# A hypergraph layer's node table that begins as a copy of x, and Newton's roots on VectorE in the node stage

## The chip, the cores and the metric

The kernel runs on one core of a Trainium2 chip. The metric is the device time of one execution in microseconds, lower is better; it is taken as the median of several runs. Engines: TensorE (PE), VectorE (DVE), ScalarE (ACT), GpSimd (POOL) and SyncE (SP). SP issues plain DMAs; POOL issues the indirect ones, which gather, scatter or add rows by an index. All of them are carried out by the core's 16 DMA engines, SP's on queue q1 and POOL's on queue q0 of the profile.

## The reference

Four graph layers stand in a row over 50,000 nodes of 256 float32 features and 25,000 edges, each with a residual and a layer norm. The change lies in the first of them, the hypergraph layer, and in the norm behind it:

```python
def _layer(x, node_idx, edge_idx, norm_n2e, norm_e2n, W_n2e, W_e2n):
    h = x @ W_n2e
    msg = norm_n2e[:, None] * h[node_idx]
    e = jax.ops.segment_sum(msg, edge_idx, num_segments=NUM_EDGES)
    e = jax.nn.relu(e)
    h2 = e @ W_e2n
    msg2 = norm_e2n[:, None] * h2[edge_idx]
    n = jax.ops.segment_sum(msg2, node_idx, num_segments=NUM_NODES)
    return (n, e)
...
Dn_inv = jnp.where(Dn > 0, 1.0 / Dn, 0.0)
norm_e2n = Dn_inv[node_idx]
x1, _ = _layer(x, node_idx, edge_idx, norm_n2e, norm_e2n, W0_n2e, W0_e2n)
x1 = jax.nn.relu(x1)
x2, _ = _layer(x1, node_idx, edge_idx, norm_n2e, norm_e2n, W1_n2e, W1_e2n)
...
x = _layernorm(x + _L0_gnn_ref(x, edge_index, ...), axis=-1)
```

So a node's value after the block is the norm of x plus the sum of its messages in the second layer, divided by the number of its edges.

## The kernel before

`hyper_layer_phase` does one hypergraph layer and runs twice, as e0 and e1. The edges lie as 128 partitions of 196 columns, J = 4 columns to a tile, so 49 tiles.

The **upward pass** takes one tick per tile. POOL gathers the source rows of four columns (L792) into g, which holds eight tiles. In e1 the rows come from the node table NS0 and carry, behind 256 features, the count of their edges; DVE's `scale` turns the count into its inverse, `inv`, in two alternating buffers, and multiplies the rows (L863 to L870). DVE's `accumulate` then runs sums of equal targets through the columns (L885), in three buffers `run`, and SP stores each finished tile (L1119). Ahead of each store SP issues clears of the node table that the layer will add into: `clear_rows` writes zeros from SBUF, 520 KB each; e1 does its 100 clears of NS1 in this way. DVE may overwrite a buffer of `run` once its store has landed, and POOL may gather into g once the tile of eight ticks before is summed.

The **downward pass** takes one tick for two columns: two products and a relu, the sums of rows with an equal source by a matmul into `pa`, ACT's copy of them into `tot` (L1080), and POOL's two indirect adds of `tot` into the node table (L822). The adds of one pair are issued when those of the pair before have landed. A row of the table is SW = 260 floats: 256 of sums, then the count. Beside the adds POOL gathers two columns of indices per tick (L832). ACT also waits for adds before it writes `tot` again, and then evicts the next product into `o` (L1089).

`first_nodes_phase`, the **node stage** (tag n0), goes over the 98 tiles of 512 nodes. Per tile SP loads the rows of x into `a` (L1201) and the rows of NS1 into `r` (L1202). DVE takes the inverse of the count (L1311, L1314), adds sums times inverse to the rows (L1319, four times), and takes row statistics (L1326). Once per two tiles it joins them into mean and variance (L1300, L1306), POOL takes the variance to the power of -0.5 (L1217), and DVE makes the shift (L1293). ACT normalises into `o` (L1269), TensorE turns the rows (L1237) and multiplies them by a weight (L1247), DVE evicts the product with a row added (L1285), and POOL scatters four times 128 rows of 2112 bytes to XH (L1223). The stages of one tile lie a fixed number of ticks apart. Every engine goes through its own instructions in program order.

Later layers of the kernel have a row norm of their own in which DVE takes the roots by Newton's steps (L2509 to L2519).

Of the kernel before, what the change touches and what calls it, by code (L numbers as in the profile page):

```python
# [5 lines left out]
F32 = mybir.dt.float32  # L6
# [6 lines left out]
P = 128  # L13
# [4 lines left out]
J = 4  # L18
# [153 lines left out]
def clear_rows(eng, table, zero, n, sem):  # L172

    eng.dma_start(table.rearrange("(p r) c -> p r c", p=P)[:, n * CLEAR:(n + 1) * CLEAR, :], zero[:]).then_inc(sem, 16)

# [508 lines left out]
def hyper_layer_phase(nc, S, tag, table, tw, sums, w1, w2, nodes, clear, up, scatter=None, listing=None, homes=None, gather=None, early=None):  # L684
# [7 lines left out]
    scaled = tw > D  # L692
    with Scope(nc, tag) as s:
# [18 lines left out]
        tot = [s.sb(f"tot{b}", [P, 2, SW]) for b in range(2)]  # L712
# [67 lines left out]
        with s.block() as block:  # L780

            @block.gpsimd
            def _(pool):
# [29 lines left out]
                for tick in range(down_ticks):  # L813
                    q = pair(tick, ADD)
                    if q:
                        pool.wait_ge(s_cp, q)
                        if q == 1:
                            pool.wait_ge(clear, 16 * CLEARS)
                        else:
                            pool.wait_ge(s_add, 32 * (q - 1))  # L820
# [18 lines left out]
            def _(dve):  # L839
# [19 lines left out]
                def scale(t):  # L859
                    gt, iv = g[:, t % RG * J:(t % RG + 1) * J, :], inv[t % 2]  # L860
                    dve.wait_ge(s_g[t % RG], 16 * J * (t // RG + 1))
                    scale_lk.settle(dve)
                    scale_lk.link(dve.tensor_scalar(iv[:], gt[:, :, D], 1.0, None, ALU.max))  # L863
                    yield
                    scale_lk.settle(dve)
                    scale_lk.link(dve.reciprocal(iv[:], iv[:]))
# [128 lines left out]
            def _(pe):  # L995
# [10 lines left out]
                for tick in range(down_ticks):  # L1006
                    q = pair(tick, SUM)
                    if q:
# [5 lines left out]
                        pe.matmul(pa[:, 0, 0:SW], e[:, 0, :], mt[:, 0, :], start=True, stop=False)  # L1014
                        pe.matmul(pa[:, 0, 0:SW], e[:, 2, :], mt[:, 1, :], start=False, stop=True)
                        pe.matmul(pa[:, 1, 0:SW], e[:, 1, :], mt[:, 1, :], start=True, stop=True).then_inc(s_tot, 1)
# [52 lines left out]
            def _(act):  # L1069
# [3 lines left out]
                for tick in range(down_ticks):  # L1073
                    q = pair(tick, COPY)
                    if q:
# [4 lines left out]
                        act.activation(tot[q % 2][:], pa[:, :, 0:SW], ACT.Copy).then_inc(s_cp, 1)  # L1080
# [27 lines left out]
            def _(sp):  # L1108
                if home:
                    home.load(sp)  # L1110
                for tick in range(up_ticks):
                    if tick < TR:
                        nodes_of, sem, n0, n1 = up
                        for n in range(n0 + (n1 - n0) * tick // TR, n0 + (n1 - n0) * (tick + 1) // TR):
                            clear_rows(sp, nodes_of, S["zero"], n, sem)
# [23 lines left out]
def first_nodes_phase(nc, S, A, T):  # L1139
# [3 lines left out]
    LD, ADD, VAR, NORM, TURN, ZT, PROD, EVICT, STORE = 0, 2, 3, 5, 6, 7, 8, 9, 10  # L1143
    RA, RR, RO = 7, 4, 7
    with Scope(nc, tag) as s:
        a = [s.sb(f"a{b}", [P, J, D]) for b in range(RA)]
        r = [s.sb(f"r{b}", [P, J, SW]) for b in range(RR)]
        o = [s.sb(f"o{b}", [P, J, XW]) for b in range(RO)]
        inv = [s.sb(f"inv{b}", [P, J]) for b in range(2)]
# [4 lines left out]
        nb = [s.sb(f"nb{b}", [P, 2 * J]) for b in range(2)]  # L1154
        zt = [s.sb(f"zt{b}", [P, KC, J, P]) for b in range(2)]
# [3 lines left out]
        s_rin = s.sems("sums_loaded", RR)  # L1159
        s_clr = s.sem("cleared")  # L1160
        s_u = s.sem("sum_ready")
# [9 lines left out]
        count_lk = Links(s.sem("count_steps"))  # L1171
# [1546 lines left out]
```

## Time and profile before

| | |
|---|---|
| median of 3 runs | 6743.85 us (6737.83 to 6748.29) |
| span of the profiled execution | 6891.4 us; no other time is given for that execution |
| busy share of the span | PE 62%, DVE 69%, ACT 48%, POOL 58% |
| DMA | 1634.06 MB, 237 GB/s over the span |
| upward pass of e1 | about 1148 to 1452 us |
| downward pass of e1 | about 1500 to 2200 us |
| node stage | about 2208 to 2860 us |

All times of the profile come from one profiled execution, whose span is 2.2% above the median of the runs. The busy share of the whole span says little here, since the stages follow one another and each has its own limit. What counts is read stage by stage: which engine or queue has no free time there.

### The profile page before, as it was taken

Reading aid. Unit: us, or ns where it says so; the run is one execution under the profiler, and the core shown is the slowest. Engines: PE = TensorE matmul, PEld = TensorE weight load, DVE = VectorE, ACT = ScalarE, POOL = GpSimd, SP = SyncE. Lnnn points to the kernel's source line nnn. Section 1 sums busy time; section 2 is a strip of 40 time slices with the busy share of each in tenths; the row PEclk is TensorE's granted clock in tenths of the full one; section 3 lists DMA queues with packets and bytes.
Section 4 is the critical chain, followed back from the end, with each engine's and each line's share of the span. In section 5 each row is a group of like instructions: output and inputs, shape, how many; then the busy total and the mean of one; then the engine's idle time right before and its main releaser. Section 6 shows DMA issues by size and latency. Waiting matters only on the chain. (4 is left out here: it accounts for less than half of the span.)

```text
span 6891.4 us, 79060 instructions
## 1 busy us (share of the span) xinstructions
PE 4257.5 (62%) x18989; PEld 3141.2 (46%) x18989; DVE 4783.1 (69%) x15487; ACT 3305.7 (48%) x7376; POOL 4010.9 (58%) x3167
## 2 busy tenths in 40 slices
PE   2568883038885788499866677988885677600000
PEld 1247773037774666377612223547774566500000
DVE  6635544645454877599599996866665999587666
ACT  0023331013332555288656665758885788633333
POOL 4757776757775788767155426611113666277776
PEclk9779996569998999799978778989998899855555
DMA  7845445864544999799688988989996677477665
GB/s 278 287 121 79 76 75 147 335 197 75 79 76 89 328 350 351 219 326 342 200 293 304 312 273 318 379 290 328 331 336 222 231 258 247 175 261 242 236 227 193
DMA packets 646111, 1634.06 MB, mean 237 GB/s; under 512 B 128454, under 2 KB 283878, under 8 KB 630290
## 3 DMA queue, kind: packets, MB, share of 16 engines
q1 hardware_dynamic: 459954, 1234.83, 51.9%
q0 software_dynamic: 185696, 394.18, 21.4%
q8 instruction: 157, 2.57, 0.2%
q14 instruction: 304, 2.49, 0.1%
HBM read 816.50 MB, written 813.62 MB: 237 GB/s over the span
## 5 line engine op out<-in xcount | busy, mean ns | idle before, releaser
L822 POOL DMA_INDIRECT NS<-e_tot,e_idx x392 | 648.6, 1655 | 298.1 <-ACT e_tot L1080 222.4
L2304 ACT ACTIVATE l_z<-l_a,l_nb,l_rs 128x256 f32<-128x256 f32 x1176 | 612.7, 605 | 411.3 <-DMA out_dram<-l_z,k_ids 248.1
L1691 POOL DMA_INDIRECT l_eg<-HBT,k_nsrc x392 | 461.8, 1178 | 391.2 <-DVEq L1916 151.3
L956 DVE TENSOR_SCALAR e_eq<-e_pk,z_skey 128x128 f32<-128x128 f32 x588 | 204.2, 348 | 637.1 <-DMA NS<-e_tot,e_idx 608.1
L2181 POOL DMA_INDIRECT out_dram<-l_z,k_ids x392 | 432.0, 1102 | 150.9 <-issue 115.1
L1734 PE MATMUL l_pb<-l_jx,k_ones 128*128 128x128 f32 x26 | 4.3, 304 | 788.3 <-DVE l_jx L1971 788.3
L1080 ACT ACTIVATE e_tot<-e_pa 128x520 f32<-128x520 f32 x196 | 118.6, 605 | 759.7 <-DMA NS<-e_tot,e_idx 748.6
L2226 PE MATMUL l_pm<-k_w_L3b,l_zt 128*128 128x258 f32 x1568 | 404.5, 417 | 126.8 <-ACT l_o L2274 121.8
L2475 DVE BATCH_NORM_STATS2 l_bs<-l_a 128x6 f32<-128x256 f32 x1176 | 467.2, 420 | 10.5 <-issue 3.5
L1223 POOL DMA_INDIRECT XH<-n_o,z_home x392 | 398.0, 1015 | 118.1 <-issue 113.1
L2342 ACT ACTIVATE l_a<-l_a,l_eshare 128x64 f32<-128x64 f32 (+1 forms) x1372 | 382.0, 371 | 124.4 <-DVE l_eshare L1953 67.6
L1911 DVE SCALAR_TENSOR_TENSOR l_erun<-l_erun,k_same,l_eg 128x260 f32<-128x260 f32 (+2 forms) x880 | 422.9, 481 | 19.2 <-DMA l_r<-XH 12.0
L2200 PE MATMUL l_ps<-l_a,k_ident 128*128 128x512 f32 x392 | 288.1, 825 | 235.0 <-DVE l_a L2449 206.5
L2226 PEld LDWEIGHTS l_pm<-k_w_L3b,l_zt 128*128 128x128 f32 x1568 | 320.6, 210 | 189.0 <-issue 138.2
L1247 PE MATMUL n_pm<-z_w_L1a,n_zt 128*128 128x264 f32 x1568 | 398.7, 411 | 12.5 <-DVE n_o L1285 12.3
L2226 PE MATMUL l_pm<-k_w_L1b,l_zt 128*128 128x264 f32 x1568 | 377.8, 395 | 26.0 <-ACT l_o L2274 25.9
L1440 POOL TENSOR_TENSOR n_rs<-n_ve,k_minus_half 128x8 f32<-128x8 f32 x49 | 80.2, 1638 | 538.4 <-DVE n_ve L1559 538.4
L2174 POOL TENSOR_TENSOR l_rs<-l_ve,k_minus_half 128x8 f32<-128x8 f32 x98 | 196.6, 2006 | 338.1 <-DVE l_ve L2499 220.3
L1031 PE MATMUL e_po<-z_w_e2n,e_hid 128*128 128x256 f32 x1584 | 381.4, 384 | 13.5 <-DVEq L919 13.5
L1691 POOL DMA_INDIRECT l_eg<-HA,k_nsrc x196 | 290.6, 1483 | 162.0 <-DVEq L1916 67.3
L1040 PE MATMUL e_pr<-e_zt,z_w_n2e 128*128 128x256 f32 x1584 | 379.6, 383 | 1.5 <-issue 1.1
L1691 POOL DMA_INDIRECT l_eg<-XH,k_psrc x196 | 299.9, 1530 | 125.9 <-DVEq L1916 66.4
(409 smaller groups left out, 13538.8 us busy)
## 6 DMA issues: line engine op xcount, KB each, us to landing
NS<-z_zero SPq DMA_DIRECT2D x200, 520.0 KB
HBT<-l_o SPq DMA_DIRECT2D x196, 528.0 KB
l_a<-HBT SPq DMA_DIRECT2D x196, 528.0 KB
GSUMS<-l_erun SPq DMA_DIRECT2D x72, 1056.0 KB
l_a<-XH SPq DMA_DIRECT2D x98, 528.0 KB
HA<-n_o SPq DMA_DIRECT2D x98, 528.0 KB
l_a<-HA SPq DMA_DIRECT2D x98, 528.0 KB
n_r<-NS SPq DMA_DIRECT2D x98, 520.0 KB
```

Of the source, the lines that this page charges most:

```text
L822: pool.indirect_dma_start(out=nodes, out_offset=bass.IndirectOffsetOnAxis(ap=idx[q % DEEP][:, k:k + 1], axis=0), in_=tot[q % 2][:, k, :], ...
L1031: mm = pe.matmul(po[:, k, :], hid[q % 2][:, i, k * P:(k + 1) * P], w2[:, i, 0:D], start=i == 0, stop=i == KC - 1)
L1040: mm = pe.matmul(pr[:, n, :], w1[:, i, n * P:(n + 1) * P], zt[q % 2][:, i].rearrange("p j n -> p (j n)"), start=i == 0, stop=i == KC - 1)
L1223: pool.indirect_dma_start(out=T["XH"], out_offset=bass.IndirectOffsetOnAxis(ap=S["home32"][:, col:col + 1], axis=0), in_=o[t % RO][:, j, : ...
L1247: last = pe.matmul(pm[h][:, i, 0:RW], zt[t % 2][:, k, h * (J // 2) + i, :], weight[:, k, :], start=k == 0, stop=k == KC - 1)
L1691: pool.indirect_dma_start(out=self.g[b % self.ng][:, k, :], out_offset=None, in_=self.table, in_offset=bass.IndirectOffsetOnAxis(ap=self.i ...
L1911: lk.link(dve.scalar_tensor_tensor(rt[:, k, 0:n], before, S["same"][:, b * BC + k:b * BC + k + 1], g[:, k, 0:n], ALU.mult, ALU.add))
L2181: pool.indirect_dma_start(out=self.out, out_offset=bass.IndirectOffsetOnAxis(ap=S["ids32"][:, col:col + 1], axis=0), in_=self.z[u % self.r ...
L2226: last = pe.matmul(self.pm[h][:, i, 0:self.wc], zt[:, k, h * (J // 2) + i, :], self.weight[:, k, 0:self.wc], start=k == 0, stop=k == KC - 1)
L2304: last = act.activation(z[:, j, 0:D], a[:, j, 0:D], ACT.Identity, bias=self.nb[b][:, col:col + 1], scale=self.rs[b][:, col:col + 1])
L2342: last = act.activation(a[:, j, f], a[:, j, f], ACT.Copy, scale=sh[:, 0, t % 2 * J + j, h:h + 1])
L2475: self.stat_lk.link(dve.bn_stats(bs[:, u % 2 * J + j, :], a[:, j, 0:D]))
```

## The change

There are two edits. First, the node table of the second hypergraph layer, NS1, has rows of 256 floats instead of 260, and it begins as x instead of as zeros: during e1's upward pass SP copies x into it (`copy_rows`, 98 DMAs from DRAM to DRAM) and clears only the spare rows. The totals are multiplied by the inverse count on ACT before they are added, in two activations instead of one, for which `inv` is kept for all tiles. So the table already holds x plus the scaled sums. The node stage then loads one tile instead of two and has no inverse and no add. Second, POOL's power leaves the node stage: DVE takes the root with a first guess and four Newton steps, thirteen dependent operations on 128x8, in a tick of their own (ROOT). The stage has one tick more from load to store, nine buffers `a` instead of seven and eight `o` instead of seven.

```diff
+def copy_rows(eng, table, x, n, sem):
+    if n == TAILN:
...
+    else:
+        eng.dma_start(table[n * BLK:(n + 1) * BLK, :].rearrange("(p j) w -> p (j w)", j=J),
+                      x[n * BLK:(n + 1) * BLK, :].rearrange("(p j) w -> p (j w)", j=J)).then_inc(sem, 16)
...
+def clear_spare_rows(eng, table, zero, sem):
+    spare = NPAD - 2 * P
+    eng.dma_start(table[spare:NPAD, :].rearrange("(p j) w -> p j w", j=2), zero[:, 0:2, 0:D]).then_inc(sem, 16)
+    eng.dma_start(table[N:N + P, :], zero[:, 0, 0:D]).then_inc(sem, 16)
...
-        inv = [s.sb(f"inv{b}", [P, J]) for b in range(2)]
+        inv = s.sb("inv", [P, TR, J]) if scaled else None
...
-                        act.activation(tot[q % 2][:], pa[:, :, 0:SW], ACT.Copy).then_inc(s_cp, 1)
+                        if scaled:
+                            for k in range(2):
+                                c = column(q) + k
+                                last = act.activation(tot[q % 2][:, k, :], pa[:, k, 0:ow], ACT.Copy, scale=inv[:, c // J, c % J:c % J + 1])
...
                         for n in range(n0 + (n1 - n0) * tick // TR, n0 + (n1 - n0) * (tick + 1) // TR):
-                            clear_rows(sp, nodes_of, S["zero"], n, sem)
+                            if x is None:
+                                clear_rows(sp, nodes_of, S["zero"], n, sem)
+                            else:
+                                copy_rows(sp, nodes_of, x, n, sem)
...
-    LD, ADD, VAR, NORM, TURN, ZT, PROD, EVICT, STORE = 0, 2, 3, 5, 6, 7, 8, 9, 10
-    RA, RR, RO = 7, 4, 7
+    LD, STAT, VAR, ROOT, SHIFT, NORM, TURN, ZT, PROD, EVICT, STORE = 0, 2, 3, 4, 5, 6, 7, 8, 9, 10, 11
+    RA, RO = 9, 8
...
-                            sp.dma_start(a[t % RA][:], A["x"][t * BLK:(t + 1) * BLK, :].rearrange("(p j) w -> p j w", j=J)).then_inc(s_in[t % RA], 16)
-                        sp.dma_start(r[t % RR][:], T["NS1"][t * BLK:(t + 1) * BLK, :].rearrange("(p j) w -> p j w", j=J)).then_inc(s_rin[t % RR], 16)
+                            sp.dma_start(a[t % RA][:], T["NS1"][t * BLK:(t + 1) * BLK, :].rearrange("(p j) w -> p j w", j=J)).then_inc(s_in[t % RA], 16)
...
-                        pool.tensor_tensor(rs[b][:], ve[b][:], S["minus_half"][:, 0:w], ALU.pow).then_inc(s_rs, 1)
...
+                def root(q):
...
+                    root_lk.settle(dve)
+                    root_lk.link(dve.tensor_scalar(y[:].bitcast(I32), v[:].bitcast(I32), -0.5, float(0x5F3759DF), ALU.mult, ALU.add))
+                    yield
+                    for n in range(4):
+                        root_lk.settle(dve)
+                        root_lk.link(dve.tensor_tensor(w[:], y[:], y[:], ALU.mult))
+                        yield
+                        root_lk.settle(dve)
+                        root_lk.link(dve.scalar_tensor_tensor(w[:], w[:], -0.5, v[:], ALU.mult, ALU.mult))
+                        yield
+                        root_lk.settle(dve)
+                        ins = dve.scalar_tensor_tensor(y[:], w[:], 1.5, y[:], ALU.add, ALU.mult)
...
-                def add(t):
-                    at, rt, iv = a[t % RA], r[t % RR], inv[t % 2]
...
-                        last = dve.scalar_tensor_tensor(at[:, j, :], rt[:, j, 0:D], iv[:, j:j + 1], at[:, j, :], ALU.mult, ALU.add)
...
-        "NS1": nc.dram_tensor("NS1", (NPAD, SW), F32).ap(),
+        "NS1": nc.dram_tensor("NS1", (NPAD, D), F32).ap(),
```

SP's instructions at the start of e1's upward pass, before the change (NS is a node table, SUMS the table of stored runs; the first row loads an index table):

```order
L577 DMA e_raw<-META 128x400
L174 DMA NS<-z_zero 128x1040 x10
L1119 DMA SUMS<-e_run 128x1024
L174 DMA NS<-z_zero 128x1040 x2
L1119 DMA SUMS<-e_run 128x1024
```

The same place after the change:

```order
L593 DMA e_raw<-META 128x400
L189 DMA NS<-z_zero 256x1x256
L190 DMA NS<-z_zero 128x256
L182 DMA NS<-in_x_dram 16x8192 x10
L1148 DMA SUMS<-e_run 128x1024
L182 DMA NS<-in_x_dram 16x8192 x2
L1148 DMA SUMS<-e_run 128x1024
```

The copies take exactly the places of the clears, two ahead of each store, and each is laid out as 16 pieces of 8192 floats, where a clear had 128 of 1040.

DVE's instructions in one tick of the node stage before the change, one in which the variance of a pair of tiles is made (n_o is the output tile, n_bs and n_mv the row statistics, n_ve the variance, n_a the rows):

```order
L1285 TENSOR_TENSOR n_o<-n_pm,z_row_a 128x2x264
L1300 BN_AGGR n_mv<-n_bs 128x2 x2
L1311 TENSOR_SCALAR n_inv<-n_r 128x4
L1285 TENSOR_TENSOR n_o<-n_pm,z_row_a 128x2x264
L1300 BN_AGGR n_mv<-n_bs 128x2 x2
L1314 RECIPROCAL n_inv<-n_inv 128x4
L1300 BN_AGGR n_mv<-n_bs 128x2 x2
L1319 SCALAR_TENSOR_TENSOR n_a<-n_r,n_inv,n_a 128x256
L1300 BN_AGGR n_mv<-n_bs 128x2 x2
L1319 SCALAR_TENSOR_TENSOR n_a<-n_r,n_inv,n_a 128x256
L1306 TENSOR_SCALAR n_ve<-n_mv 128x8
L1319 SCALAR_TENSOR_TENSOR n_a<-n_r,n_inv,n_a 128x256 x2
```

DVE in a tick of the node stage after the change, one of those with a root (n_rs is the root, n_sq its scratch):

```order
L1299 TENSOR_TENSOR n_o<-n_pm,z_row_a 128x2x264
L1318 TENSOR_SCALAR n_rs<-n_ve 128x8
L1351 BN_STATS n_bs<-n_a 128x6
L1299 TENSOR_TENSOR n_o<-n_pm,z_row_a 128x2x264
L1322 TENSOR_TENSOR n_sq<-n_rs 128x8
L1351 BN_STATS n_bs<-n_a 128x6
L1325 SCALAR_TENSOR_TENSOR n_sq<-n_sq,n_ve 128x8
L1351 BN_STATS n_bs<-n_a 128x6
L1328 SCALAR_TENSOR_TENSOR n_rs<-n_sq,n_rs 128x8
L1351 BN_STATS n_bs<-n_a 128x6
L1322 TENSOR_TENSOR n_sq<-n_rs 128x8
L1325 SCALAR_TENSOR_TENSOR n_sq<-n_sq,n_ve 128x8
```

The adds and the inverse are gone. The root's steps alternate with evictions and statistics as long as there are some; the last nine of the thirteen follow one another directly (two of them are shown). On POOL the 49 powers between every eight scatters of the stage are gone, and its 392 scatters follow one another.

## Rows read from the trace of the kernel before

**Rows 1.** Busy time by stretch: PE, PEld, DVE, ACT, POOL, clock, DMA share, GB/s.

```profile
1148.00:1452.00 304.00, 1.80 (x4) 1.01 (x4) 192.74 (x573) 0.00 (x0) 212.47 (x199) 0.50 0.91 346
1500.00:2200.00 700.00, 582.37 (x2908) 495.13 (x2908) 343.70 (x1767) 236.61 (x486) 506.94 (x368) 0.97 0.47 72
2300.00:2750.00 450.00, 366.48 (x1760) 300.45 (x1758) 355.68 (x1250) 229.64 (x441) 362.62 (x331) 0.93 0.98 350
```

**Rows 2.** Timeline of POOL, node stage: the first and the last scatter.

```profile
2259.07 1.06 POOL L1223 DMA_INDIRECT XH<-n_o,z_home  x1 [0.18 <-issue]
...
2854.88 0.97 POOL L1223 DMA_INDIRECT XH<-n_o,z_home  x1 [0.30 <-issue]
```

**Rows 3.** Groups of instructions, 2300 to 2750: busy us, mean ns, idle before.

```profile
L1223 POOL DMA_INDIRECT XH<-n_o,z_home x294 | 299.6, 1019 | 85.3 <-issue 84.6 <-ACT n_o L1269 0.5 <-DVE n_o L1285 0.2
L1217 POOL TENSOR_TENSOR n_rs<-n_ve,k_minus_half 128x8 f32<-128x8 f32 x37 | 63.6, 1718 | 2.4 <-issue 1.4 <-DVE n_ve L1306 0.5
...
L1319 DVE SCALAR_TENSOR_TENSOR n_a<-n_r,n_inv,n_a 128x256 f32<-128x256 f32 x292 | 126.6, 476 | 1.3
L1285 DVE TENSOR_TENSOR n_o<-n_pm,z_row_a 128x528 f32<-128x528 f32 x147 | 103.3, 703 | 90.5 <-PE n_pm L1247 48.3 <-remote 25.1 <-issue 17.0
L1311 DVE TENSOR_SCALAR n_inv<-n_r 128x4 f32<-128x4 f32 x73 | 11.9, 163 | 0.0
L1314 DVE RECIPROCAL n_inv<-n_inv 128x4 f32<-128x4 f32 x73 | 11.5, 157 | 0.0
```

**Rows 4.** Timeline of TensorE in the node stage, at full clock.

```profile
2519.59 3.73 PE L1247 MATMUL n_pm<-z_w_L1a,n_zt 128*128 128x264 f32 x16
...
2524.30 3.73 PE L1247 MATMUL n_pm<-z_w_L1a,n_zt 128*128 128x264 f32 x16
```

**Rows 5.** Timeline of POOL, downward pass: first add of three pairs.

```profile
1698.74 1.76 POOL L822 DMA_INDIRECT NS<-e_tot,e_idx  x1 [0.52 <-ACT e_tot L1080]
...
1705.62 1.76 POOL L822 DMA_INDIRECT NS<-e_tot,e_idx  x1 [0.49 <-ACT e_tot L1080]
...
1713.15 1.62 POOL L822 DMA_INDIRECT NS<-e_tot,e_idx  x1 [1.15 <-ACT e_tot L1080]
```

**Rows 6.** DMA queues, 1262 to 1355 (93 us): packets, MB, share of 16 engines.

```profile
q1 hardware_dynamic: 7982, 29.36, 78.6%
q0 software_dynamic: 3141, 8.72, 23.8%
```

**Rows 7.** DMA queues, node stage, 2300 to 2750.

```profile
q1 hardware_dynamic: 21186, 77.75, 53.7%
q0 software_dynamic: 23450, 79.29, 43.8%
```

**Rows 8.** Groups of DVE, 6000 to 6600: Newton's steps in a later layer.

```profile
L2516 DVE SCALAR_TENSOR_TENSOR l_rt<-l_rt,l_ve 128x8 f32<-128x8 f32 x128 | 20.9, 163 | 10.5 <-DVE l_rt L2513 4.4 <-issue 2.9 <-remote 1.9
L2513 DVE TENSOR_TENSOR l_rt<-l_rs 128x8 f32<-128x8 f32 x128 | 20.8, 163 | 18.1 <-remote 10.9 <-DVE l_rs L2519 5.7
L2519 DVE SCALAR_TENSOR_TENSOR l_rs<-l_rt,l_rs 128x8 f32<-128x8 f32 x128 | 20.8, 162 | 16.9 <-remote 9.3 <-DVE l_rt L2516 6.2
...
L2509 DVE TENSOR_SCALAR l_rs<-l_ve 128x8 int32<-128x8 int32 x32 | 6.4, 201 | 11.2 <-issue 11.2
```

**Rows 9.** Timeline, start of the node stage: the last memset of `a`.

```profile
2216.67 0.91 DVE L1278 MEMSET n_a<- 128x1024 f32 x1 [0.16 <-issue]
```

**Rows 10.** Groups of ACT, downward pass, 1500 to 2200.

```profile
L1089 ACT ACTIVATE e_o<-e_po,z_einv_end 128x256 f32<-128x256 f32 x196 | 82.3, 471 | 65.2 <-DVEq L934 51.3 <-PE e_po L1031 10.5 <-issue 3.4
L1080 ACT ACTIVATE e_tot<-e_pa 128x520 f32<-128x520 f32 x98 | 59.3, 605 | 378.4 <-DMA NS<-e_tot,e_idx 372.8 <-PE e_pa L1016 5.6
```

**Rows 11.** Waits of ACT and of POOL, 1500 to 2200: total, times, longest.

```profile
ACT e_o L1089 <- DVEq L934: 51.3, 89, 1.1
...
POOL NS L822 <- ACT e_tot L1080: 106.1, 87, 27.4
```

**Rows 12.** DMA queue of the adds and index gathers, 1600 to 2100.

```profile
q0 software_dynamic: 25186, 19.11, 36.4%
```

More of the change, by code:

```diff
@@ L711, in hyper_layer_phase @@
         idx = [s.sb(f"idx{b}", [P, 2], I32) for b in range(DEEP)]
-        tot = [s.sb(f"tot{b}", [P, 2, SW]) for b in range(2)]
+        tot = [s.sb(f"tot{b}", [P, 2, ow]) for b in range(2)]
         pt = [s.ps(f"pt{b}", [P, KC, 2, P]) for b in range(2)]
@@ L1112, in _ @@
                     if tick < TR:
-                        nodes_of, sem, n0, n1 = up
+                        nodes_of, sem, n0, n1, x = up
+                        if x is not None and tick == 0:
+                            clear_spare_rows(sp, nodes_of, S["zero"], sem)
                         for n in range(n0 + (n1 - n0) * tick // TR, n0 + (n1 - n0) * (tick + 1) // TR):
-                            clear_rows(sp, nodes_of, S["zero"], n, sem)
+                            if x is None:
+                                clear_rows(sp, nodes_of, S["zero"], n, sem)
+                            else:
+                                copy_rows(sp, nodes_of, x, n, sem)
                     t = tile(tick, 4)
@@ L1154, in first_nodes_phase @@
         nb = [s.sb(f"nb{b}", [P, 2 * J]) for b in range(2)]
+        sq = [s.sb(f"sq{b}", [P, 2 * J]) for b in range(2)]
         zt = [s.sb(f"zt{b}", [P, KC, J, P]) for b in range(2)]
@@ L1208, in _ @@
                 for tick in range(ticks):
-                    q = pair(tick, VAR)
-                    if q is not None:
-                        q, w = q
-                        b = q % 2
-                        pool.wait_ge(s_var, q + 1)
-                        if q >= 2:
-                            pool.wait_ge(s_nb, q - 1)
-                            pool.wait_ge(s_z, 2 * (q - 1))
-                        pool.tensor_tensor(rs[b][:], ve[b][:], S["minus_half"][:, 0:w], ALU.pow).then_inc(s_rs, 1)
                     t = tile(tick, STORE)
@@ L1332, in _ @@
                         parts.append(evict(tick - EVICT))
-                    q = pair(tick - 1, VAR)
+                    q = pair(tick, SHIFT)
                     if q is not None:
                         parts.append(shifts(q[0]))
+                    q = pair(tick, ROOT)
+                    if q is not None:
+                        parts.append(root(q[0]))
                     q = pair(tick, VAR)
@@ L1338, in _ @@
                         parts.append(variance(*q))
-                    if tile(tick, ADD) is not None:
-                        parts.append(add(tick - ADD))
+                    if tile(tick, STAT) is not None:
+                        parts.append(stats(tick - STAT))
                     take_turns(parts)
```

61 lines of the change are left out of this document (30 added, 31 removed).

## The prediction

> **What bounds the kernel now.** I began with the busy time by stretch, to separate the three stages that the change touches [rows 1]. In the row 1148 to 1452 (upward pass of the second hypergraph layer) TensorE does nothing and the DMA engines are 91% busy at 346 GB/s. In 1500 to 2200 (its downward pass) they are 47% busy and TensorE 83%. In 2300 to 2750 (the middle of the node stage) they are 98% busy at 350 GB/s. The three stages have three different limits.
>
> In the node stage a tile's pace comes from the first and the last scatter of POOL: from 2259.07 to 2854.88 us there are 391 intervals, so 595.8 / 391 x 4 = 6.095 us for a tile of four scatters [rows 2]. POOL has no free time in it. Its scatters follow one another after 0.30 us that wait for nothing ("issue"), and once per pair of tiles a power of 1.7 us stands between them, with 0.18 behind it, as before the first scatter: 1.88 us a pair. Over 2300 to 2750 the groups say the same: 299.6 + 85.3 us for 294 scatters and 63.6 + 2.4 for the powers are 450.9 of 450 us [rows 3]. ACT's wait for a scatter to land is the stage backing up behind POOL and the DMA engines. So two limits lie on each other here: POOL's own work, and DMA at 98%. TensorE is behind them: at full clock one tile's products start 4.71 us after the last tile's (2519.59, 2524.30) [rows 4].
>
> In the downward pass POOL issues two adds into the table and two small gathers for each pair of columns: 1698.74 to 1705.62 is 6.88 us with 0.49 us of gap before the next pair's first add, and sometimes the adds of the pair before land late and the gap is 1.15 us [rows 5]. In the upward pass the DMA engines are the limit where it runs well: in 1262 to 1355 they move 410 GB/s, and the two data queues together take 102% of them [rows 6].
>
> **The change, node stage: fewer loads, no power on POOL.** Of each tile's three streams one goes, the 520 KB load of sums. The queue q1 took 53.7% of 16 engines for 450 us to move 77.75 MB, and the scatters' q0 43.8% for 79.29 MB [rows 7]. That is 0.537 x 7200 / 77.75 = 49.7 engine-us per MB to load and 39.8 to store. A tile now needs 0.52 MB of loads and 1.08 MB of scatters: (26.1 + 43.0) / 16 = 4.3 us. DMA is out of the way. POOL loses 1.88 / 2 = 0.94 us per tile; what stays is four scatters, 4 x (0.97 + 0.30) = 5.08 at the undisturbed length and 4 x (1.019 + 0.30) = 5.28 at the mean that a full DMA system gives [rows 2, 3]. I take 5.2.
>
> Does VectorE allow that? It was busy 355.7 us for 73.7 tiles, 4.83 us each [rows 1]. Out go four adds (0.476 us by the group; four in a row took 1.67 in the timeline) and the count's two small operations (0.32, of which about 0.1 lies on neighbours): about 1.9. In come thirteen dependent operations on 128x8 per pair of tiles. The layers later in the program run the same chain, so its price is in the trace: 20.9 + 20.8 + 20.8 + 6.4 us busy, and 10.5 + 18.1 + 16.9 + 11.2 us idle before them, for 32 pairs, is 125.6 / 32 = 3.9 us per pair, 1.95 per tile [rows 8]. Sum 4.83 - 1.9 + 1.95 = 4.9 us, just under POOL's 5.2. The order above shows that the last nine of these operations stand alone, with nothing to fill the waits between them; without any waits (13 x 0.163 = 2.1 per pair) VectorE would need 4.0, so 4.0 to 4.9. TensorE's 4.71 fits too; where its clock falls (0.93 on average in rows 1) it needs 4.71 / 0.93 = 5.06. Everything is within 0.5 us of the same pace, which is why I don't go below 5.2.
>
> Term one: (6.095 - 5.2) x 97.75 tiles = -87. Against it, about +4: two more of the 0.91 us memsets ahead of the first load, each with 0.16 before it [rows 9], and a first pass that is one tick deeper, whose chain of 3.9 stands in place of 1.7. Node stage: **-83 us**.
>
> **Downward pass.** ACT writes the totals in two activations of 128x256 instead of one of 128x520. Two such back to back are in the trace as the evictions at line 1089, 0.471 each by the group, so 0.94 at most in place of 0.605, +0.34 us [rows 10]. ACT then waits for DVE 0.58 us at a time anyway (51.3 us in 89 times) before its next work [rows 11], and POOL needs this copy only one pair later. I cost it at nothing; with that cover gone it would be 98 x 0.34 = +33. The added rows shrink from 1040 to 1024 bytes. POOL's issue doesn't depend on that as far as any row shows. What could gain is the landing: POOL waited 106.1 us in 87 times, 27.4 of it once at the start, so 0.92 each for the rest, against the 0.49 of rows 5 where POOL came from other work; at most 0.43 x 86 = -37. I take **-5**, a seventh, since most pairs in rows 5 are POOL's own work.
>
> **Upward pass: clears become copies.** This is the term on which the sign hangs. 100 clears of 520 KB from SBUF become 98 copies of 512 KB from DRAM to DRAM, and two small clears of 262 and 131 KB. As the order shows, each copy is 16 pieces of 32 KB, one per engine, on SP's queue, two ahead of each store of runs. Stores wait behind copies in that queue, VectorE waits for stores after three tiles, and POOL for VectorE after eight. So nothing defers them past the stage.
>
> Price of a clear now: in rows 6 q1 took 0.786 x 1488 / 29.36 = 39.8 engine-us per MB, so 0.5325 x 39.8 / 16 = 1.33 us of all engines; 100 are 133. Price of a copy: the trace has none. From below, it can't be cheaper than the store leg alone, 0.524 x 39.8 / 16 = 1.31. From above, if the engine does its read leg and then its write leg, at the node stage's rates, (49.7 + 39.8) x 0.524 / 16 = 2.93. Only the adds into the table read DRAM and write it in one packet, with 1040-byte rows: they look dear (36.4% of 8000 engine-us for 19.11 MB, 152 per MB, four times a store [rows 12]), but they also read a second source and come in small rows, so they bound nothing above; they only say that the cheap end is not to be assumed. I take 2.4: two store legs (2.62) with a little overlap. Then 98 x 2.4 = 235, less 133: +102 us of DMA time. The stage has 9% of 304 us idle [rows 1], 27 us, into which the excess spreads since loads run up to eight tiles ahead: **+75 us**.
>
> The Trainium skill has a figure against this part: DMA: Bandwidth & Descriptors, Latency and other measured facts, gives copies between HBM tensors as 207 to 214 GB/s per direction at their full rate. By an estimate from that figure a copy is 2.45 us and the sum 5 us higher than mine. No row of this trace shows a DRAM-to-DRAM copy.
>
> **Sum.** -83 - 5 + 75 = -13 on a profiled span of 6891.4 us, which is 2.2% above the median of the runs, 6743.85; no separate time of the profiled execution is given. Scaled or not, that is -13: 6730 us. A measurement of this kernel tells 0.2%, 13.5 us, from no change.
>
> **Rivals.**
> (1) The two halves nearly cancel, the forecast: a copy at 2.2 to 2.65, node pace 5.1 to 5.4. Stage +55 to +100, node -63 to -92: 6690 to 6775. Chance 0.50.
> (2) The copy is nearly as cheap as a clear, at 1.31 to 1.8 us: reads and writes overlap in an engine. For it: q1's loads and stores use the same engines at 50 and 40, no engine shows a second limit. Stage -5 to +16, so 6640 to 6675. Chance 0.32.
> (3) The other side: read leg and write leg in turn, 2.93 us. 98 x 2.93 - 133 = 154 of DMA time, less 27: +127, sum +39: 6783. It decides from the price at which 98 x - 160 = 88, that is 2.53 us, and is measurably slower from 2.67. Its place is SP's queue, where run stores stand behind copies. Chance 0.12.
> (4) VectorE bounds the node stage: the lone chain costs 3.9 us per pair on top of evictions that wait on TensorE, pace 5.7. Node -35, sum +35: 6779. For it: VectorE's evictions already wait for TensorE in rows 3 (48.3 us). Against: those waits are slack in a stage that POOL holds back. Chance 0.06.
>
> **The numbers.** In (1) the centre is at -13, so about half lies below -13.5, a third within, a sixth above. Faster: 0.32 + 0.23 = 0.55 less 0.03 for (2) meeting (4), 0.52. Within 0.2%: 0.18. Slower: 0.30. The range that leaves out 2 in 10 is 6650 to 6785; (1) alone has 6690 to 6775.
>
> **What would show it.** The first scatter to the last, 391 intervals, should be 508 us (5.2 a tile), POOL's idle still "issue", DMA share about 0.83 and VectorE about 4.9 us per tile. The upward pass should last about 380 us rather than 304, with DMA near 1.0 throughout and q1 at 73 engine-us per MB on copies. The adds of the downward pass should keep their 6.9 us. I am wrong if the upward pass keeps its length (rival 2), passes 430 us (3), or if POOL waits for VectorE in the node stage (4).

## The result and the profile after

The changed kernel took 6634.14 us (median of 4 runs, 6632.3 to 6637.03) against 6743.44 us before: ratio 0.9832, 95% interval 0.9818 to 0.9846. The forecast was 6730, range 6650 to 6785. So 109 us were gained where 13 were forecast. The experiments added a limit to this: on two other chips, where the kernel before takes 6872 and 6885 us, the changed kernel is no faster at all (last section).

The profile shown ahead of the prediction has a span of 6891.4 us, 2.2% above its median. A second profile of the kernel before, `before_again` (span 6727.6), is used for differences. It was taken later than the profile after, in the session of the first experiments, whose kernel before took 6738.19 us. By stage, first to last instruction of its kind, in us:

| stage | before_again | after | difference | forecast |
|---|---|---|---|---|
| e1 upward pass (first gather to last run) | 276.9 | 276.2 | -0.7 | +75 |
| e1 downward pass (adds) | 667.1 | 669.8 | +2.7 | -5 |
| first memset of `a` to first scatter | 48.2 | 35.5 | -12.7 | +4 |
| first to last scatter of the node stage | 594.2 | 504.4 | -89.8 | -87 |
| everything before e1's upward pass | | | +8 | 0 |
| everything from the next layer's first gather | 3974.9 | 3972.4 | -2.6 | 0 |

The spans differ by 93.9 us. The +8 ahead of the upward pass is no effect of the change: `copy_only` and `double_copy`, which have the same code up to there as after, begin that pass at 1092.5 and 1095.9 us, after at 1102.0 and before_again at 1094.3. The busy time by stretch (columns as in [rows 1]) of the kernel after, for the upward pass, the downward pass and the middle of the node stage:

```profile
1102.00:1378.00 276.00, 0.59 (x2) 0.50 (x2) 187.19 (x572) 0.00 (x0) 209.77 (x199) 0.50 0.99 375
1500.00:2100.00 600.00, 493.90 (x2480) 419.64 (x2478) 296.65 (x1529) 220.34 (x500) 452.77 (x329) 0.98 0.47 72
2300.00:2600.00 300.00, 269.95 (x1406) 227.71 (x1405) 228.33 (x1022) 182.52 (x349) 229.11 (x233) 0.98 0.90 306
```

The same three stretches in before_again:

```profile
1094.00:1371.00 277.00, 0.59 (x2) 0.50 (x2) 187.02 (x572) 0.00 (x0) 210.21 (x199) 0.50 0.99 379
1500.00:2100.00 600.00, 488.48 (x2436) 413.69 (x2434) 292.65 (x1510) 197.83 (x408) 447.80 (x325) 0.97 0.48 71
2300.00:2600.00 300.00, 242.75 (x1167) 200.41 (x1168) 235.18 (x824) 151.19 (x292) 241.65 (x220) 0.93 0.98 347
```

The upward pass has the same length and the same DMA share, 0.99, with copies as with clears, and the GB/s differ by no more than the bytes (512 KB a piece of work for 520). The DMA queues between 1150 and 1350 say it directly (packets, MB, share of 16 engines; compare [rows 6]); first after, then before_again:

```profile
q1 hardware_dynamic: 7629, 57.94, 71.5%
q0 software_dynamic: 7080, 19.53, 29.3%
```

```profile
q1 hardware_dynamic: 15555, 57.22, 71.3%
q0 software_dynamic: 7105, 19.63, 28.9%
```

Half the packets, the same bytes, the same share. 0.715 x 3200 / 57.94 = 39.5 engine-us per MB, copies and stores mixed, where the prediction had 73 for copies. The packet records of the two traces agree: a copy's 32768-byte packet takes 1214 ns (median of 1552), a clear's 4160-byte one 161 ns, which is 27.0 and 25.8 bytes per ns. All packets of the 97 full copies together took 125.5 us of 16 engines, 1.29 us a copy.

In the node stage POOL's scatters of after, the first and the last (timeline; they answer to [rows 2]):

```profile
2149.87 1.04 POOL L1237 DMA_INDIRECT XH<-n_o,z_home  x1 [44.83 <-DVE n_o L1299]
...
2654.27 0.98 POOL L1237 DMA_INDIRECT XH<-n_o,z_home  x1 [0.30 <-issue]
```

That is 504.4 / 391 x 4 = 5.16 us a tile. The groups of POOL and of VectorE in after, 2300 to 2600 (columns as in [rows 3]):

```profile
L1237 POOL DMA_INDIRECT XH<-n_o,z_home x233 | 229.5, 985 | 71.0 <-issue 66.4 <-DVE n_o L1299 4.6
```

```profile
L1299 DVE TENSOR_TENSOR n_o<-n_pm,z_row_a 128x528 f32<-128x528 f32 x117 | 82.6, 706 | 63.7 <-PE n_pm L1261 63.3
L1339 DVE BATCH_NORM_AGGREGATE n_mv<-n_bs 128x2 f32<-128x6 f32 x238 | 27.7, 159 | 0.0
L1328 DVE SCALAR_TENSOR_TENSOR n_rs<-n_sq,n_rs 128x8 f32<-128x8 f32 x116 | 19.2, 165 | 3.0
L1325 DVE SCALAR_TENSOR_TENSOR n_sq<-n_sq,n_ve 128x8 f32<-128x8 f32 x116 | 18.9, 163 | 3.0
L1322 DVE TENSOR_TENSOR n_sq<-n_rs 128x8 f32<-128x8 f32 x116 | 18.6, 160 | 2.0
...
L1318 DVE TENSOR_SCALAR n_rs<-n_ve 128x8 int32<-128x8 int32 x29 | 5.8, 200 | 0.0
```

POOL's 229.5 + 71.0 us fill the 300. It waits for VectorE for 4.6 us only. VectorE still waits 63.3 us for TensorE. Its Newton chain costs 62.5 us busy and 8 idle for 29 pairs, 2.4 us a pair.

### The profile page after: what moved, and what is told of

The parts are those of the page before. It is cut to its first block and busy times, and to the rows that moved or that the text cites. A ratio compares the mean times of both kernels' runs of the same rounds, so it can differ in the third digit from the quotient of the medians.

```text
span 6633.7 us, 78919 instructions
## 1 busy us (share of the span) xinstructions
PE 4192.1 (63%) x18989; PEld 3106.0 (47%) x18989; DVE 4681.3 (71%) x15539; ACT 3316.8 (50%) x7474; POOL 3866.4 (58%) x3118
## 5 line engine op out<-in xcount | busy, mean ns | idle before, releaser
L2209 POOL DMA_INDIRECT out_dram<-l_z,k_ids x392 | 417.8, 1066 | 119.6 <-issue 113.5
L1719 POOL DMA_INDIRECT l_eg<-HA,k_nsrc x196 | 271.6, 1386 | 177.8 <-DVEq L1944 86.8
L1261 PE MATMUL n_pm<-z_w_L1a,n_zt 128*128 128x264 f32 x1568 | 367.2, 388 | 0.0
L1499 PE MATMUL n_pm<-k_w_L3a,n_zt 128*128 128x264 f32 x1568 | 364.8, 386 | 0.0
```

The source lines that it names most:

```text
L1261: last = pe.matmul(pm[h][:, i, 0:RW], zt[t % 2][:, k, h * (J // 2) + i, :], weight[:, k, :], start=k == 0, stop=k == KC - 1)
L1719: pool.indirect_dma_start(out=self.g[b % self.ng][:, k, :], out_offset=None, in_=self.table, in_offset=bass.IndirectOffsetOnAxis(ap=self.i ...
L2209: pool.indirect_dma_start(out=self.out, out_offset=bass.IndirectOffsetOnAxis(ap=S["ids32"][:, col:col + 1], axis=0), in_=self.z[u % self.r ...
```

## The experiments

Each run is compared with the kernel before on its own chip; "us a tile" is the pace of the node stage's scatters. The first four ran on a chip whose kernel before took 6738.19 us; the changed kernel was not timed there.

**before_again**, the kernel before once more:

> The unchanged kernel of before, to have a profile whose span fits its time: the first profile had a span of 6891 us against a median of 6744, the changed kernel's 6634 against 6634. Theory: the first profiled execution was a disturbed one and this one shows about 6742 us, with the 150 us gone from all stages a little, among them the slow stretches at 1200 to 1262 and 1355 to 1390 us of the upward pass. With them gone that pass should take about 270 to 285 us and the node stage keep 6.1 us per tile. Rival: the profiler itself lengthens this kernel, and the span is again near 6890.

6729.27 us. The theory held: the upward pass took 276.9 us, the node stage 6.08 us a tile. It supplied the columns above.

**root_only**: the kernel before with the Newton root alone; both loads, the inverse and the adds stay.

```diff
-    LD, ADD, VAR, NORM, TURN, ZT, PROD, EVICT, STORE = 0, 2, 3, 5, 6, 7, 8, 9, 10
-    RA, RR, RO = 7, 4, 7
+    LD, ADD, VAR, ROOT, SHIFT, NORM, TURN, ZT, PROD, EVICT, STORE = 0, 2, 3, 4, 5, 6, 7, 8, 9, 10, 11
+    RA, RR, RO = 8, 4, 7
...
-                        pool.tensor_tensor(rs[b][:], ve[b][:], S["minus_half"][:, 0:w], ALU.pow).then_inc(s_rs, 1)
...
+                        parts.append(root(q[0]))
```

> Before, with the roots of the node stage on VectorE and nothing else changed (second load, adds, clears as before). Theory of two limits on each other: POOL has 0.94 us less per tile, but the DMA engines still need their 5.9 us for it, so the pace falls from 6.1 to 5.9 or 6.0: 10 to 15 us faster, 6730. Rival, POOL alone was the limit: pace 5.2 and 85 us faster, 6658. A third: VectorE, which keeps its adds (4.83 us) and gets the chain (1.95), is the limit at 6.8: 65 us slower.

6661.35 us, ratio 0.9883 (0.9864 to 0.9901). The scatters took 522.0 us, 5.34 a tile, 72 less than before, with as many bytes per tile. Its stretch 2300 to 2600, and POOL's only group there:

```profile
2300.00:2600.00 300.00, 262.51 (x1348) 218.87 (x1349) 297.13 (x1323) 176.64 (x339) 229.64 (x225) 1.00 1.02 401
```

```profile
L1216 POOL DMA_INDIRECT XH<-n_o,z_home x225 | 231.0, 1026 | 70.7 <-issue 70.7
```

The rival "POOL alone was the limit" (6658) came within 4 us, and the theory of two limits missed by 69 us. The same DMA engines that were 98% busy at 347 GB/s now move 401 GB/s. So a share of 98% in before was no limit, and POOL's power held the stage. VectorE is busy 297 of 300 us, and POOL's scatters with their gaps are 301.7: here both are at their end.

**copy_only**: the changed kernel with the root back on POOL.

```diff
+                        pool.tensor_tensor(rs[b][:], ve[b][:], S["minus_half"][:, 0:w], ALU.pow).then_inc(s_rs, 1)
...
-                        parts.append(root(q[0]))
```

> After, with the power back on POOL: only the copy, the scaled totals and the single load of the node stage. Theory of two limits: POOL needs 4 x 1.285 + 0.94 = 6.08 us per tile, as before, so the node stage gains nothing, and the whole change less this is 5 to 15 us faster than before (6730 to 6738), from the upward pass. Rival, the DMA engines alone were the limit: pace 5.2, 90 us faster.

6696.28 us, ratio 0.994 (0.9921 to 0.9958). Neither theory had this: the one of two limits expected no gain in the node stage and at least 6730 us, its rival 90 us. Scatters 573.9 us, 5.87 a tile; from memset to first scatter 37.9 us where root_only has 48.5. POOL's groups, 2300 to 2600:

```profile
L1246 POOL DMA_INDIRECT XH<-n_o,z_home x204 | 200.2, 982 | 59.2 <-issue 58.0 <-ACT n_o L1292 0.6 <-DVE n_o L1308 0.6
L1240 POOL TENSOR_TENSOR n_rs<-n_ve,k_minus_half 128x8 f32<-128x8 f32 x25 | 42.2, 1687 | 0.3
```

The scatter falls from 1030 ns in before_again to 982: one load less is worth 0.05 us per scatter, 0.2 a tile (20 us), and a fill that is 10 us shorter. The two edits alone give -77 and -42 us here; together they gave -109 by the medians of the first measurement, 10 less than the sum.

**double_copy**: every copy is issued a second time, into a table that nobody reads.

```diff
                                 copy_rows(sp, nodes_of, x, n, sem)
+                                copy_rows(sp, up[5], x, n, sem)
```

> After, with each copy of 512 KB issued a second time, into a table that nobody reads. It prices the copy itself in the upward pass. Theory: a copy from DRAM to DRAM takes an engine no longer than a store of the same bytes, 1.21 to 1.27 us for its 32 KB; with 2% idle in that pass the 98 more cost 98 x 1.27 less about 6 us, +118, so 6752. Rival (what the prediction took): a copy costs about 2.4 us of the engines, hidden in after by slack: +235, 6869.

6755.56 us, ratio 1.0023 (1.0008 to 1.0039). That is the time of the theory (6752), and 121 us above the median of the changed kernel in the first measurement. The upward pass took 405.3 us, its stretch:

```profile
1096.00:1501.00 405.00, 0.59 (x2) 0.50 (x2) 183.99 (x572) 0.00 (x0) 207.48 (x199) 0.50 0.99 382
```

98 more copies cost 129.1 us, 1.32 us each, and everything else of the stage is unchanged (POOL 207 us busy for 210, VectorE 184 for 187). This is the price that the prediction lacked, measured in place: the cost of the store leg alone (1.31), and 524288 bytes in 1.32 us are 397 GB/s of data copied.

The next four ran on a second chip, where the kernel before took 6882.1 us.

**zeros_again**: the copies replaced by 512 KB stores of zeros from SBUF.

```diff
-        eng.dma_start(table[n * BLK:(n + 1) * BLK, :].rearrange("(p j) w -> p (j w)", j=J),
-                      x[n * BLK:(n + 1) * BLK, :].rearrange("(p j) w -> p (j w)", j=J)).then_inc(sem, 16)
+        eng.dma_start(table[n * BLK:(n + 1) * BLK, :].rearrange("(p j) w -> p (j w)", j=J), zero[:].rearrange("p r c -> p (r c)")[:, 0:J * D]).then_inc(sem, 16)
```

> After, with each of the 97 full copies replaced by a store of 512 KB of zeros from SBUF into the same place (so x is left out of the output), 128 pieces of 4096 bytes each; nothing else changes. Theory that a copy from DRAM to DRAM costs the engines what a store costs: 97 x (1.27 - 1.31) is -4, the same within 6 us as after. Rival (copies cost more and the upward pass hides it): the upward pass falls from 276 us to about 265.

6884.34 us, ratio 1.0004 (0.9988 to 1.0021); upward pass 301.1 us, node stage 6.36 a tile.

**small_pieces**: each copy as 128 pieces of 4096 bytes instead of 16 of 32768.

```diff
+        pieces = lambda t: t[n * BLK:(n + 1) * BLK, :].rearrange("(a b k) w -> b a (k w)", a=2, k=J)
+        eng.dma_start(pieces(table), pieces(x)).then_inc(sem, 16)
```

> After, with each copy cut into 128 pieces of 4096 bytes instead of 16 of 32 KB, by an access pattern that doesn't merge. Theory that only bytes count: a piece takes 0.159 us as a load or store of its size does, 1.27 us of an engine per copy, upward pass 276 us as before, total the same within 6 us. Rival: the cheap copy comes from its long pieces, and short ones pay for reading and writing DRAM, 0.2 to 0.3 us a piece: 30 to 100 us slower. A lesser rival: long pieces hold up the gathers, and short ones gain 5 us.

6888.08 us, ratio 1.0009 (0.9991 to 1.0026); upward pass 304.7, node stage 6.39. The size of the pieces does nothing that the times can tell. The packets say more: in this pass 17,991 of 4096 bytes are recorded, two thirds of them pieces of copies and the rest stores of runs, and their median is 159 ns, the first theory's number.

**unread_load**: a second load of 512 KB per tile into two buffers that nobody reads.

```diff
+                            if t >= RR:
+                                sp.wait_ge(s_rin[t % RR], 16 * (t // RR))
+                            sp.dma_start(r[t % RR][:], A["x"][t * BLK:(t + 1) * BLK, :].rearrange("(p j) w -> p j w", j=J)).then_inc(s_rin[t % RR], 16)
```

> After, with a second load per tile again in the node stage: 512 KB of x into two spare buffers that nobody reads. Theory from root_only, where the engines moved 401 GB/s, while before they moved 346 at a share of 97%: the share counts packets that wait, and was no limit. 2.12 MB at 400 GB/s is 5.3 us per tile against 5.16: 0 to 15 us slower. Rival, the prediction's: at 98% the DMA engines were at their limit with 2.13 MB per tile, 5.9 us: 75 us slower.

6897.33 us, ratio 1.0023 (1.001 to 1.0036); node stage 6.39.

**copies_early**: all copies moved to the first layer's downward pass, two behind each load of stored runs.

```diff
+                        for k in (2 * n, 2 * n + 1):
+                            copy_rows(sp, begin[0], begin[1], k, begin[2])
```

> After, with the 98 copies moved from the upward pass of the second layer, where the engines are 98% busy, to the downward pass of the first, where they are 47% busy: two behind each load of runs on SP's queue. Theory: the upward pass falls from 276 us to what POOL's 196 gathers need, 196 x 1.3 = 255, or a little above, and the downward pass, bound by POOL's issue, stays: 12 to 20 us faster, 6616. Rival: pieces of 32 KB delay the landing of the adds by up to 1.2 us in pairs where they meet, and POOL waits for the landing: up to 98 x 0.6 = 60 us slower in the downward pass, 40 in all.

7028.43 us, ratio 1.0213 (1.0189 to 1.0236). The adds of that downward pass took 812.5 us against 666 to 678 in the other profiles, far more than even the rival had. The upward pass, now without copies, still took 301.0 us. POOL's adds there, 500 to 1200, wait for ACT's totals (which wait for earlier adds to land) 190.0 us before 164 adds; first copies_early, then after, 500 to 1100:

```profile
L840 POOL DMA_INDIRECT NS<-e_tot,e_idx x164 | 271.8, 1657 | 215.8 <-ACT e_tot L1103 190.0 <-issue 25.7
```

```profile
L840 POOL DMA_INDIRECT NS<-e_tot,e_idx x172 | 284.2, 1652 | 112.2 <-ACT e_tot L1103 82.9 <-issue 26.2 <-DMA NS<-e_tot,e_idx 3.1
```

The DMA share there rises only from 0.47 to 0.53. Free share doesn't make a place free: ACT waits for earlier adds to land for 446.0 us before 82 totals, 5.4 us each, in after 344.4 before 85, 4.1 each. A later try gave the same.

None of these four gave the time that either theory had for a chip like the first, because the changed kernel itself gains nothing there. So four runs went to a third chip (before 6871.87 us).

> The changed kernel again, unchanged, together with the kernel of before. The last four runs fell on another chip, on which the kernel of before takes 6882 us instead of 6738, and kernels that should equal the changed one took as long as before (ratio 1.000 and 1.001) with a node stage of 622 us instead of 504. Theory: such a chip delays the handing over between engines now and then (up to 8 us at once, node stage 6.4 us per tile), and the gain of the change is lost there: ratio 0.983 on a chip with before near 6740, about 1.000 on one with before near 6880. Rival: the four kernels themselves were slow, and this one has a ratio of 0.983 on any chip.

> The kernel of before again, for its profile on the same chip as after_2. On a chip with before near 6740: a span of about 6730, node stage 594 us, upward pass 277. On one near 6880: span near 6880, upward pass 300 as in the first profile, node stage 595 to 620.

> After with a second load per tile that nobody reads, as unread_load, whose chip hid the answer. Theory, the share of 98% was no limit: on a chip with before near 6740 the node stage takes 504 to 520 us, total 0 to 15 us above after_2. Rival, the DMA engines were at their limit with 2.13 MB per tile: 75 us slower. On the other chip both give a few us.

> After with the copies in the first layer's downward pass, as copies_early, which cost that pass 140 us and saved nothing in the upward pass on the other chip. On a chip with before near 6740: if pieces of 32 KB delay the landing of the adds, the downward pass again takes about 810 us instead of 671 (1.4 us per pair), and the upward pass, freed of copies, shows its other limit: 255 to 262 us if it was bound by the engines, 276 if it was not. Total 100 to 130 us slower than after_2.

after_2: 6865.29 us, ratio 0.9997 (0.9981 to 1.0013). before_2: 6869.87. unread_load_2: 6865.45, ratio 0.9996 (0.998 to 1.0012). copies_early_2: 7002.47, ratio 1.0202 (1.0176 to 1.0227), its adds 818.8 us and the upward pass, now without copies, 282.7 instead of 302.8: 20 us gained, and 144 lost in the adds (674.9 in after_2). after_2 decides for its theory: the gain is lost on such a chip. The unread load cost nothing there (6865.45 for 6865.29), but the question that it was made for, a chip like the first, wasn't met in any of its three runs.

The last four ran on a fourth chip (before 6884.9 us), to separate the copies from the rest once more and to ask whether TensorE's work makes the node stage slow there. **half_product** leaves out one of the two matmuls of each product:

```diff
-                                for k in range(KC):
+                                for k in range(1):
...
-                                                     start=k == 0, stop=k == KC - 1)
+                                                     start=k == 0, stop=True)
```

> The changed kernel again, beside the three others. If this chip is like the first (kernel before near 6740 us): 6634 us, ratio 0.984, node stage 5.16 us a tile. If it is like the two others (before near 6875): ratio 1.000, node stage 6.3 us a tile.

> The changed kernel with the copies of x replaced by stores of zeros from SBUF (x is missing in the result). Theory 1 (a copy costs what a store costs): equal to after_3 within 10 us. Theory 2 (copies cost more and something else hides it): 20 us or more faster.

> The changed kernel with a second load of 512 KB per tile that nobody reads. Theory 1 (POOL's own work set the pace of the node stage before, the DMA share of 98% was no limit): within 10 us of after_3, pace within 0.1 us a tile. Theory 2 (DMA bound too): on a chip like the first the pace goes back to 5.9 us or more, 70 us slower than after_3.

> The changed kernel with one of the two matmuls per 128 rows left out of the node stage's product (the second half of the features isn't multiplied), so TensorE does about 2.9 us per tile instead of 4.7 there; loads, evictions, scatters and POOL's work stay. Theory 1 (TensorE's own load or its clock makes the hand-overs late where the node stage takes 6.3 us a tile): on such a chip the stage falls to about 5.2 us a tile, 100 us less than after_3. Theory 2 (the delays come from outside TensorE): it stays above 6.0 us. On a chip like the first both say 5.1 to 5.2 us, the same as after_3, since POOL sets the pace.

| | us | ratio (95%) | upward pass | us a tile |
|---|---|---|---|---|
| after_3 | 6889.32 | 1.0008 (0.9997 to 1.002) | 302.7 | 6.38 |
| zeros_2 | 6887.53 | 1.0001 (0.9989 to 1.0013) | 301.5 | 6.38 |
| unread_load_3 | 6907.99 | 1.0031 (1.0018 to 1.0043) | 304.1 | 6.43 |
| half_product | 6900.09 | 1.0015 (1.0004 to 1.0026) | 306.9 | 6.46 |

Zeros against copies on one chip: 1.8 us apart in all and 1.2 in the upward pass, as theory 1 of zeros_2 says (a copy costs what a store costs), by a control that changes nothing else. Alone it is a weak one: with a DMA share of 0.91 that pass has some 27 us in which a copy 0.3 us dearer than a store could hide (an estimate from 303 us and 98 copies), and copies_early_2 shows that leaving all copies out saves only 20 us on such a chip. It does exclude 2.4 us. The unread load kept the pace within 0.1 us, but cost 19 us in all where at most 10 were expected; theory 2 had no number for this kind of chip. half_product refutes the part of its theory 1 on TensorE's load: with the matmul time cut from 239 to 179 of 300 us, the pace isn't better. The part on the clock it doesn't test, since the granted clock fell from 0.93 to 0.76 in that stretch instead of rising.

## Why the prediction was wrong

**The step that failed** is "I take 2.4: two store legs (2.62) with a little overlap", and with it "Upward pass: +75". A copy costs 1.32 us of all engines; the term is 98 x 1.32 less 133, -4 us, and 0 (-0.7) was measured. The lower bound of the prediction, 1.31, was the value, and rival 2 the case that came, "reads and writes overlap in an engine". double_copy and the queue and packet rows of after show it independently, and zeros_2 agrees. The sum with 0 in that place, -83 - 5, is 6656 us, and the range began at 6650. What took the time below the range is the fill, 17 us better than forecast, and the pace of the node stage, 3 us better, against a downward pass 8 us worse: the four stage differences measured add up to -100.5, which is 6643. Rival 2's own span, 6640 to 6675, misses 6634 by 6 us for the same reason.

The choice of 2.4 leaned on the adds of [rows 12], "the cheap end is not to be assumed", though the same paragraph said they bound nothing. For the bound above, 2.93, loads at 50 and stores at 40 engine-us per MB in [rows 7] were added as if legs were served in turn. The measured copy, 39.5 in a mix with stores, is as cheap as the store leg alone. Nor were those figures all work: before_again booked 0.98 x 16 x 6.08 = 95 engine-us for a tile, root_only with the same loads and scatters 1.02 x 16 x 5.34 = 87. The Trainium skill (DMA: Bandwidth & Descriptors, Latency and other measured facts) gives 207 to 214 GB/s per direction for copies between HBM tensors of tiles of 128 rows of 16 KiB that lie far apart. The contiguous copies here ran at 397 in double_copy, so the 2.45 us estimated from that figure are not borne out for them. The span of rival 1 was not added up strictly either: its terms with the -5 give 6702 to 6776, where 6690 to 6775 is written. That doesn't change the outcome.

**Idle time to absorb it, 27 us**: not there on the chip of the first experiments. The 9% of [rows 1] belong to a profile whose upward pass was 25 us longer than before_again's; in before_again DMA is at 0.99, 3 us idle. With a dear copy the term would have been larger still.

**Node stage, -83**: right in mechanism and nearly in size. Pace 5.2 predicted, 5.16 measured; 391 intervals 504.4 for 508; POOL's idle is "issue". But "two limits lie on each other" was half wrong: root_only shows that POOL's own work held the stage (-72 of -90), and the load's part is the shorter scatter (-20). The 1.88 us per pair would be 92 us; 72 came. Part of the difference is the gap: before_again's timeline has 0.20 us before the scatter behind a power and 0.30 before every other, so one gap grew as the power went. The DMA share of after is 0.90 where 0.83 was expected, at 306 GB/s for 347. **VectorE 4.9 us a tile**: 3.93 busy (228.33 us for 58.1 tiles). The chain costs 2.4 us a pair, not 3.9. The 3.9 came from the long profile: the same lines of the later layer in before_again, 5836 to 6436, for [rows 8]:

```profile
L2519 DVE SCALAR_TENSOR_TENSOR l_rs<-l_rt,l_rs 128x8 f32<-128x8 f32 x122 | 19.6, 161 | 1.5
L2516 DVE SCALAR_TENSOR_TENSOR l_rt<-l_rt,l_ve 128x8 f32<-128x8 f32 x123 | 19.6, 159 | 1.5
L2513 DVE TENSOR_TENSOR l_rt<-l_rs 128x8 f32<-128x8 f32 x123 | 19.4, 158 | 1.6
```

The twelve steps behind the first guess have 4.6 us of idle time where [rows 8] had 45.5. Rival 4 fell with that. **Fill, +4**: measured -12.7. The memsets and the deeper pass are there, but the copy's edit makes the fill shorter: copy_only alone has 37.9 us, root_only 48.5. Of that, VectorE's wait for its first rows accounts for little (3.6 us for 4.9); how the rest divides, the missing add and inverse in the first ticks above all, is argued and not measured. This was the second largest miss.

**Downward pass, -5**: the adds took 669.8 for 667.1, no gain. The two activations are hidden, as said: ACT, groups of 1500 to 2100 in after, for [rows 10]:

```profile
L1101 ACT ACTIVATE e_tot<-e_pa,e_inv 128x256 f32<-128x256 f32 x174 | 72.9, 470 | 348.2 <-DMA NS<-e_tot,e_idx 348.2
L1113 ACT ACTIVATE e_o<-e_po,z_einv_end 128x256 f32<-128x256 f32 x166 | 69.6, 470 | 27.4 <-DVEq L952 27.4
```

0.47 us each, and much of the longer copy came out of ACT's wait for VectorE, which fell from 46.2 us in 81 times in before_again to 27.4 in 82 in the same stretch. Two or three microseconds either way are no effect: over the 18 profiles these adds take 664 to 675 us.

By the medians the gain is 109 us, by the profiles 94: the profiled execution of before_again took 6729.27 us, 14 less than the median of the kernel before (6743.44), while that of after took 6635.44, its median.

## What to carry to other kernels

A DRAM-to-DRAM copy can be priced like a store of as many bytes where the DMA engines are full (1.32 for 1.31 us here); when a cost has no row and its lower bound is a clean mechanism, give that bound its full chance, and don't add legs. Read a DMA share near 1 together with its GB/s: if the same engines move more elsewhere in the trace (410 in [rows 6] against 350 in [rows 7]), they need not be at their limit. A profile whose span is 2% above the median has other idle times than the kernel that is timed, and two terms of this prediction were read from such times (the 27 us and the chain's 3.9). A change is worth timing on more than one chip.

## What was not expected of the hardware

**The gain isn't there on every chip.** Where the kernel before took 6743 us the changed one was 1.7% faster, and where it took 6738 the two parts alone gave 1.2% and 0.6%. Where it takes 6872 to 6885 (three of the four chips of the experiments; the changed kernel was timed on two of them) it is the same. Each chip was used in one session, so chip and session can't be told apart. The profile ahead of the prediction looks like those of the slow chips, though its kernel's median was 6744: DMA share 0.91 at 346 GB/s in the upward pass, and waits released by "remote" in the node stage [rows 1, 3], of which before_again has none. The two kernels' stretches on the third chip, before_2 and then after_2:

```profile
1130.00:1432.00 302.00, 0.58 (x2) 0.50 (x2) 191.51 (x573) 0.00 (x0) 210.03 (x199) 0.50 0.91 348
2300.00:2600.00 300.00, 241.45 (x1172) 200.59 (x1171) 236.91 (x827) 153.67 (x294) 239.91 (x219) 0.93 0.97 348
```

```profile
1133.00:1436.00 303.00, 0.81 (x3) 0.72 (x4) 191.60 (x572) 0.00 (x0) 210.09 (x199) 0.50 0.91 341
2300.00:2600.00 300.00, 235.65 (x1127) 187.31 (x1128) 182.32 (x828) 146.00 (x287) 185.99 (x189) 0.94 0.74 254
```

The kernel before hardly feels it in the node stage (604.5 us for 594.2), the changed one has 614.9 for 504.4: 0.74 DMA share and a POOL with 114 us idle (71 in after). Nobody is busy all the time. The waits of after_3 in the same stretch (total, times, longest):

```profile
ACT n_zt L1273 <- remote: 109.0, 20, 9.1
DVE n_o L1299 <- PE n_pm L1261: 63.4, 30, 4.4
POOL XH L1237 <- DVE n_o L1299: 63.2, 30, 4.7
```

One such place in its timeline, start, us, instruction, and the wait before it:

```profile
2407.66 2.05 PE L1261 MATMUL n_pm<-z_w_L1a,n_zt 128*128 128x264 f32 x8 [0.35 <-DVE n_o L1299]
...
2410.09 1.09 PE L1251 MATMUL n_pt<-k_ident,n_o 128*128 128x128 f32 x8 [0.38 <-ACT n_o L1283]
...
2412.79 0.71 DVE L1299 TENSOR_TENSOR n_o<-n_pm,z_row_a 128x528 f32<-128x528 f32 x1 [3.74 <-remote]
...
2413.64 5.20 PE L1261 MATMUL n_pm<-z_w_L1a,n_zt 128*128 128x264 f32 x16 [2.46 <-DVE n_o L1299]
...
2414.36 1.02 ACT L1273 ACTIVATE n_zt<-n_pt 128x1024 f32<-128x1024 f32 x1 [4.32 <-remote]
...
2415.78 0.98 POOL L1237 DMA_INDIRECT XH<-n_o,z_home  x1 [2.55 <-DVE n_o L1299]
```

TensorE's records end at 2409.71 and 2411.18; VectorE and ACT, which by the program wait for these, go on 3.1 and 3.2 us later, and POOL then has nothing to scatter. The profile models the ends of matmuls, so part of the delay may lie in TensorE's own last products. ACT has 20 such waits in 300 us, of up to 9.1 us. Delays aren't confined to TensorE's products either: POOL's gap that waits for nothing, 0.30 us at most in after, reaches 1.7 us in after_3's node stage and 2.2 in its upward pass. Before the change ACT spends 102.9 us of this stretch (before_2) waiting for scatters to land, so there is slack behind POOL; in after_2 it waits for none, and POOL waits 57.2 us for VectorE instead. That the slack hides the delays before and its absence shows them after is a reading of these rows; no run tested it by adding slack. What makes the hand-overs late stays open: less work for TensorE doesn't cure it (half_product), nor do the copies matter (zeros_2), and the upward pass, in which TensorE does nothing, is 25 us longer on these chips as well. The DMA engines alone don't hold that pass there: without any copy it took 301.0 and 282.7 us, at a share of 0.55 and 0.59.

**DMA share above 1.** root_only's node stage is booked at 1.02 of 16 engines and moves 401 GB/s, 16% more than before_again at 0.98. So the time that packets take isn't all work: some of it overlaps or is waiting. Which of the two, no row shows.
